# Part of a scan stage's front for batch 0 placed between the steps of the preceding stage's last chain

## The reference, cut to what matters

```python
# delta attention: 16 heads of 32, per head a state S (32 x 32)
pred = einsum('bhk,bhkv->bhv', kt, S)
delta = bt[..., None] * (vt - pred)
S = S + einsum('bhk,bhv->bhkv', kt, delta)
o = einsum('bhk,bhkv->bhv', qt, S)
...
og = o * gate, scaled per head by its rms; return og @ Wo.T

# selective scan: its first input is ctx_1024 (4, 512, 256), the gate z is the decoder's x
x = einsum('bld,ed->bel', hidden_states, in_proj_w)           # 256 -> 512 channels
xc = conv_general_dilated(x, conv_w, ...)                      # causal, 4 taps, per channel
x = silu(xc + conv_b)
dt_low, Bm, Cm = split(einsum('bdl,ed->bel', x, x_proj_w), [16, 32], axis=1)
dt = softplus(einsum('brl,dr->bdl', dt_low, dt_proj_w) + dt_proj_b)
state = state * exp(d * A) + (d * u) * b;  y = sum over 16 states of state * c
y = (y + D * x) * silu(z)
```

## Time and profile before

| what | value |
|---|---|
| median of 3 runs | 3259.52 us (3243.12 to 3270.23) |
| the profiled execution: its time, its span | 3257.45 us, 3255.7 us |
| its mean granted TensorE clock | 0.903 of full speed |
| busy over the span: PE, DVE, ACT, POOL | 82%, 59%, 44%, 35% |
| end of the last chain, from the span's start | 779.4 us |
| first scanned group of the scan | 860.4 us |

### The profile page before, as it was taken

The page is one execution under the profiler, slowest core; times in us unless marked ns, Lnnn a source line. Parts: engine busy times, 40 slices in busy tenths (PEclk is TensorE's granted clock), DMA queues, the critical chain, the costliest instruction groups (busy, mean ns, idle before and its releaser), DMA issues.

```text
span 3255.7 us, 50521 instructions
## 1 busy us (share of the span) xinstructions
PE 2679.7 (82%) x20154; PEld 1457.2 (45%) x20154; DVE 1923.6 (59%) x2994; ACT 1430.0 (44%) x2575; POOL 1130.8 (35%) x1056
## 2 busy tenths in 40 slices
PE   5788878876676766679998989888877999999788
PEld 3565655654222322248864544444443334333244
DVE  3323232333589899975735565665755666677377
ACT  3232333220544555433235445453622665666455
POOL 0443334440466666530005342526214233322000
PEclk8888898887888888789999999999887999999899
DMA  2222222230312314032244232333417444543301
GB/s 88 73 53 67 55 62 67 60 88 14 123 50 74 111 39 156 14 141 81 80 131 131 102 102 77 104 114 88 152 52 145 102 116 94 138 87 79 119 27 40
DMA packets 196766, 284.50 MB, mean 87 GB/s; under 512 B 84388, under 2 KB 86468, under 8 KB 195636
## 3 DMA queue, kind: packets, MB, share of 16 engines
q1 hardware_dynamic: 196532, 281.27, 29.5%
HBM read 192.08 MB, written 63.31 MB: 78 GB/s over the span
## 4 chain that ended last, share of the span: by engine, by line
PE 38%; DVE 9%; issue 4%; ACT 4%; POOL 2%; DMA 2%; SPq 1%; DVEq 0%; ACTq 0%; POOLq 0%
PE ps L236 8%; PE ps L3388 4%; PE ps L3401 4%; PE ps L1846 4%; PE ps L1857 4%; PE ps L3320 3%; PE ps L3337 2%; PE ps L3371 2%; PE ps L2512 1%; PE ps L3325 1%; DVE arena L2775 1%; DVE arena L1434 1%; DMA arena<-arena 1%; PE ps L2520 1%; DVE arena L2773 1%
## 5 line engine op out<-in xcount | busy, mean ns | idle before, releaser
L236 PE MATMUL ps<-arena 128*128 128x512 f32 (+3 forms) x1296 | 480.9, 525 | 16.1 <-ACT arena L2612 6.1
L3573 DVE TENSOR_REDUCE cross<-ps 128x1 f32<-128x512 f32 x512 | 327.6, 685 | 176.3 <-PE ps L3371 176.2
L1466 POOL TENSOR_TENSOR arena<-arena 128x1024 f32<-128x1024 f32 x128 | 311.1, 2431 | 193.1 <-DVE arena L1458 193.1
L3481 ACT ACTIVATE cross<-ps 128x512 f32<-128x512 f32 x512 | 276.7, 592 | 149.5 <-PE ps L3388 149.3
L1482 PE MATMUL ps<-arena 128*128 128x512 f32 x512 | 266.6, 661 | 56.6 <-POOL arena L1466 56.4
L1458 DVE TENSOR_TENSOR_SCAN arena<-ps,arena 128x1024 f32<-128x1024 f32 x128 | 291.3, 2277 | 33.1 <-ACT ps L1449 33.1
L236 PEld LDWEIGHTS ps<-arena 128*128 128x128 f32 (+2 forms) x1296 | 194.4, 155 | 254.0 <-issue 178.2
L1449 ACT ACTIVATE ps<-arena 128x511 f32<-128x511 f32 x256 | 165.1, 679 | 188.1 <-DVE arena L1458 187.9
L576 POOL TENSOR_TENSOR arena<-arena 128x31 f32<-128x31 f32 (+15 forms) x217 | 130.2, 600 | 324.6 <-DMA arena<-d_a 308.1
L1482 PEld LDWEIGHTS ps<-arena 128*128 128x128 f32 x512 | 104.4, 212 | 213.2 <-issue 125.5
L3388 PE MATMUL ps<-cross,cross 50*128 50x512 f32 x512 | 156.2, 505 | 28.4 <-ACT cross L3481 22.8
(11 more groups left out here) (351 smaller groups left out, 5171.2 us busy)
## 6 DMA issues: line engine op xcount, KB each, us to landing
arena<-d_bc SPq DMA_DIRECT2D x32, 1024.0 KB, 5.3
cross<-d_parts SPq DMA_DIRECT2D x192, 128.0 KB, 4.4
arena<-d_x SPq DMA_DIRECT2D x16, 1024.0 KB, 5.5
d_parts<-cross SPq DMA_DIRECT2D x32, 512.0 KB, 3.8
d_x<-arena SPq DMA_DIRECT2D x48, 256.0 KB, 2.7
arena<-in_D_wlm SPq DMA_DIRECT2D x12, 1024.0 KB, 6.4
d_signs<-arena SPq DMA_DIRECT2D x32, 256.0 KB, 2.2
arena<-arena SPq DMA_DIRECT2D x64, 128.0 KB, 2.1
```

The costliest lines, as they stand in the source:

```text
L236: ins = pe.e.matmul(ps[:m, :n], lhsT(k), rhs(k), start=(k == 0), stop=(k == chunks - 1))
L1466: pool.e.tensor_tensor(h, h, s.bc[:, turn % s.SLOTS, 1], ALU.mult).then_inc(*pool.up("scan_hC"))
L3481: act.e.activation(s.E[:, k % 2, j], s.rexp.bank((u, i)), ACT.Exp).then_inc(*s.rexp.empty(act, (u, i)))
L3573: dve.e.tensor_reduce(s.mx[:, u % 2, t, h:h + 1], s.rmax.bank((u, m)), AX.X, ALU.max, negate=True).then_inc(*s.rmax.empty(dve, (u, m)))
```

## The change

The scan's front of batch 0 (input projection, convolution, silu, and the projection to dt, B and C) moves out of the scan stage into Delta's last iteration. Each engine gets a `..._front` function of the scan: PE's is the generator that fills the last chain. It has 26 matmuls of 512 columns for the projection and convolution, an empty place, and 4 matmuls for dt, B and C: 31 pieces for 31 places. ACT's runs after `act_og` of pair 6, DVE's (the four multiplications with the taps) before the last chain, POOL's (the convolution of block 0) after its last inverse, SP's after the last `sp_inverse`: it stores the B and C rows and loads the first 3 of the 8 row pairs. The banks for these results come out of Delta's ring. So that the weights are there, `sp_next` is issued one iteration earlier, ahead of the last inverse's transfer. The buffers of the scan are laid out anew, so that those written early lie where Delta no longer reads. The gate's silu of batch 0 moves on ACT from ahead of the softplus to after the decay of group 2.

```diff
+            last = p == self.PAIRS - 1
+            if last:
+                yield from ((("in", c), "act") for c in range(2))
             if back:
                 yield ("o", p, 0), "dve"
             if front:
                 yield from ((("G", n, h), "act") for h in range(2))
                 yield from ((("PT", n, e), "dve") for e in range(2))
+            if last:
+                yield from ((("in", c), "act") for c in range(2, C))
+                yield ("xd",), "act"
...
-                s.sp_next(sp, s.dead, [s.ring.at_filled(sp, ("PT", s.PAIRS - 1, s.E - 1))])
+                s.next.sp_front(sp, s.ring)
...
                 for k in s.pieces(n):
                     s.sp_piece(sp, k)
+                if n == s.PAIRS - 1:
+                    s.sp_next(sp, s.dead, [s.ring.at_filled(sp, ("PT", n, s.E - 1))])
                 s.sp_inverse(sp, n)
...
+        s.next.pool_front(pool, s.ring, s.ring.at_filled(pool, ("PT", s.PAIRS - 1, s.E - 1)))
...
-            fill = s.pe_fill(pe, n) if front else iter(())
+            fill = s.pe_fill(pe, n) if front else s.next.pe_front(pe, s.ring) if p < s.PAIRS else iter(())
             if back:
                 s.pe_chain(pe, p, fill)
...
                 s.act_og(act, p - 1)
+            if p == s.PAIRS - 1:
+                s.next.act_front(act, s.ring)
             if front:
                 s.act_split_k(act, n)
...
                 s.dve_og_scale(dve, p - 1)
+            if p == s.PAIRS - 1:
+                s.next.dve_front(dve)
             if front:
                 s.dve_k_unit(dve, n)
...
+    def sp_front(self, sp, ring):
+
+        s = self
+        sp.e.wait_ge(*ring.at_emptied(sp, ("xd",)))
+        sp.e.dma_start(s.io["d_bc"][0].rearrange("a n l -> (a n) l"), s.xd[s.R:s.R + 2 * s.N, :]).then_inc(*sp.up("scan_bc_kept", 16))
+        for g in range(s.EARLY_ROWS):
+            s.sp_rows(sp, 0, g)
+        sp.b = 0
+
+    def pool_front(self, pool, ring, dead):
+
+        s = self
+        pool.e.wait_ge(*dead)
         pool.e.memset(s.up[:, :, 0:s.pad], 0.0).then_inc(*pool.up("scan_zeros"))
         pool.e.memset(s.ctx[:, :, 0:s.pad], 0.0).then_inc(*pool.up("scan_zeros"))
+        pool.e.wait_ge(*pool.at_all("scan_zeros"))
+        pool.e.wait_ge(*pool.at_all("scan_weights"))
+        pool.e.wait_ge(*ring.at_emptied(pool, ("in", 0)))
+        for k in range(s.K):
+            s.pool_tap(pool, 0, 0, k)
+        for k in range(1, s.K):
+            s.pool_add_tap(pool, 0, 0, k)
+        pool.b = 0
+
+    def pe_front(self, pe, ring):
+
+        s, e = self, pe.e
+        pe.e.wait_ge(*pe.at_all("scan_weights"))
+        pe.e.wait_ge(*pe.on("scan_ctx", 0))
+        for c in range(C):
+            pe.e.wait_ge(*ring.at_free(pe, ("in", c)))
+            if c == s.PE_CONV[0]:
+                pe.e.wait_ge(*pe.at_all("scan_taps"))
+                pe.e.wait_ge(*pe.at_all("scan_zeros"))
+            taps = (None,) if c in s.POOL_CONV else range(s.K)
+            for tap in taps:
+                for k in range(s.CC):
+                    if tap is None:
+                        lhsT, rhs = s.wi[:, k, c * P:(c + 1) * P], s.ctx[:, k, s.pad:]
+                    else:
+                        at = P * s.PE_CONV.index(c)
+                        lhsT, rhs = s.wk[:, tap, k, at:at + P], s.ctx[:, k, tap:tap + L]
+                    last = tap in (None, s.K - 1) and k == s.CC - 1
+                    ins = e.matmul(ring.bank(("in", c)), lhsT, rhs, start=(tap in (None, 0) and k == 0), stop=last)
+                    if last:
+                        ins.then_inc(*ring.fill(pe, ("in", c)))
+                    yield
+        yield
+        pe.e.wait_ge(*ring.at_free(pe, ("xd",)))
+        m = s.R + 2 * s.N
+        for c in range(C):
+            pe.e.wait_ge(*pe.on("scan_u", 0, c + 1))
+            ins = e.matmul(ring.bank(("xd",))[:m], s.wx[:, c, :], s.u[:, 0, c, :], start=(c == 0), stop=(c == C - 1))
+            if c == C - 1:
+                ins.then_inc(*ring.fill(pe, ("xd",)))
+            yield
+
+    def act_front(self, act, ring):
+
+        s = self
+        for c in range(C):
+            act.e.wait_ge(*ring.at_filled(act, ("in", c)))
+            dst = s.up[:, c, s.pad:] if c in s.POOL_CONV else s.dt[:, 0, c]
+            act.e.activation(dst, ring.bank(("in", c)), ACT.Copy).then_inc(*ring.empty(act, ("in", c)))
+        for c in range(C):
+            if c in s.POOL_CONV:
+                act.e.wait_ge(*act.on("scan_pool_conv", 0, s.POOL_CONV.index(c) + 1))
+            else:
+                act.e.wait_ge(*ring.at_emptied(act, ("in", c)))
+            act.e.activation(s.u[:, 0, c, :], s.dt[:, 0, c, :], ACT.Silu, bias=s.cb[:, c:c + 1]).then_inc(*act.up("scan_u"))
+        m = s.R + 2 * s.N
+        act.e.wait_ge(*ring.at_filled(act, ("xd",)))
+        act.e.activation(s.xd[:m, :], ring.bank(("xd",))[:m, :], ACT.Copy).then_inc(*ring.empty(act, ("xd",)))
+        act.b = 0
+
+    def dve_front(self, dve):
+
+        s = self
+        dve.e.wait_ge(*dve.at_all("scan_weights"))
+        for k in range(s.K):
+            dve.e.tensor_tensor(s.wk[:, k], s.wk[:, k], s.wi[:, :, P * s.PE_CONV[0]:], ALU.mult).then_inc(*dve.up("scan_taps"))
...
-        s.sp_keep_bc(sp, 0)
-        for g in range(s.G):
+        for g in range(s.EARLY_ROWS, s.G):
             s.sp_rows(sp, 0, g)
...
-        for c in s.POOL_CONV:
-            for k in range(s.K):
-                s.pool_tap(pool, 0, c, k)
-            for k in range(1, s.K):
-                s.pool_add_tap(pool, 0, c, k)
         s.pool_floor(pool, 0, 0)
         s.pool_dt(pool, 0, 0)
...
-        for c in range(C):
-            s.act_up(act, 0, c)
-        s.act_u(act, 0)
-        s.act_gate(act, 0)
-        s.act_xd(act, 0)
         s.act_abs(act, 0, 0)
         s.act_ln(act, 0, 0)
...
-                if b and k == 7:
+                if k == (7 if b else 1):
...
-        for c in range(C):
-            for half in (0, 1) if c in s.PE_CONV else (None,):
-                s.pe_in(pe, 0, c, half)
-        s.pe_xd(pe, 0)
         s.pe_dt(pe, 0, 0)```

On PE the last chain changes like this, from the transposes of pair 6 to the third step. Before:

```order
L679 MATMUL ps<-arena 128x128 x8
L777 MATMUL ps<-arena 128x128 x2
L767 MATMUL ps<-arena 32x128 x2
L777 MATMUL ps<-arena 128x128 x2
L767 MATMUL ps<-arena 32x128 x2
L777 MATMUL ps<-arena 128x128 x2
```

## The result

The changed kernel takes 3231.68 us (median of 6 runs, 3223.12 to 3235.8) against 3257.89 us for the kernel before (6 runs, 3243.12 to 3270.23): ratio 0.9919, 95% interval 0.9893 to 0.9945. That is 26 us, where 31.8 were forecast; the forecast ratio of 0.9902 lies inside the interval. The profiled execution of the changed kernel has a span of 3229.9 us, 25.8 less than before.

The account below looks back on a forecast made before the run. Strictly sequential stages bound the kernel, so time saved between last chain and first scan comes off the end; -35.2 + 1.0 + 4.8 + 0.5 - 2.9 = -31.8 us from 3259.52 gives 3228 us, range 3212 to 3245.

Parts of the forecast that it names:

- The front: Batch 0's work ahead of the first scan, taken out of the scan stage: first scan at 825.2 instead of 860.37, -35.2 us.
- The chain: Last chain on PE with matmuls in its gaps: 2.92 us a step, +1.0 per output, +4.8 us in all.
- rival (a): Before and in last chain: issue wait stays (+2.9), inverse's transfer queues (+2), chain starts at slow clock (+2.8); 3235.5 us, 22%.
- Rival (b): Last chain: filled, it never leaves the slow clock, 5.7 us a step, +43 us, time 3271 us; chance 5%.
- The early weights: Ahead of the last chain: weights issued before the inverse's transfer, +0.5 us for its queueing, -2.9 us for PE's issue wait.
- The stall's term: Line 669 in pair 7's triangles: PE's 5.26 us issue wait falls to 2.4 once the weights' traffic is gone, -2.9 us.
- The inverse's queueing: Pair 7's inverse transfer may wait behind the early weights' traffic: +0.5 us taken, bounds 0 and 3.
- The gate: ACT after decay 2: table load and silu take 3.2 us, 2.3 of it slack, so +1.0 us.
- Rival (c): More comes back: line 669 finds its instructions there (-2.4), output projection keeps the busier chain's clock (-2.6); 3223 us, 11%.

## Why the prediction was right

- **The front is worth 35 us, not its 27 us of matmuls.** Right, by the right mechanism. The next late thing was named (`wdt` behind the store of batch 3, then the slow matmul), and it came at 818.38: 9.5 us behind the output projection, 9.3 forecast, and took 2.04 us, 1.97 forecast. The experiment that removes it gives 8.1 us.
- **The chain.** The price per step was exact: 12 steps and three outputs from 736.86 to 774.90 are 38.0 us, by the forecast's numbers 12 x 2.92 + 3.0 = 38.0. Mis-sized were its ends: the first fill cost 1.6 us instead of 1.0, since it met the slow clock (1.91 us at 733.64), and the steps with the projection took 7.0 us for two where 6.2 were forecast. That slow first fill is all that came of rival (a)'s slow start of the chain, 0.6 of its 2.8 us. Rival (b), a chain that stays at the slow clock, is out: 1.00 from the first update on.
- **The early weights.** The stall's term was slightly small. Its cause, PE waiting for instructions that the weights hold up, fits the place of the instruction packet in all eleven traces. The Trainium skill (Runtime: NRT & Kernel Launch, Instruction fetch mechanics) has instruction fetch hidden, and by that the sum would have been -28.9 us. The traces differ from it: the stall follows the transfer's place in both directions, 5.26 to 2.12 us and 1.61 to 4.58. The inverse's queueing was +1.7 in this trace, more than the 0.5 taken and within the bound of 3, and mostly absent in others: the first part of rival (a) is out, its second happens now and then.
- **The gate.** The +1.0 for ACT's delay is seen in the kernel with the gate behind the logarithm. In the changed kernel the announced wait of DVE for ACT did not come; the step missed that a logarithm 3 us later meets POOL's instruction, and at group 3 the delay was 2.4 us. That only 0.6 of it was left at the end was not foreseen either, so that this term is near its forecast by luck. The sentence that DVE is busy without a gap from the first scan was wrong: it waits for ACT ahead of 12 scans of the stage, 33.1 us in all before and 32.4 after. ACT in turn waits for PE at some of these, and there a delay as well as a gain is partly taken back.
- **Rival (c)** did not come: 1.61 us of stall stayed, and the output projection took 16.12 us, 0.5 less than before, with the same idle time ahead of it. In the other traces it took 15.62 to 16.82 us with a filled chain or without, so even these 0.5 us need not be the change's.

The terms missed by -0.5, +1.2, -0.7, +1.4 and -0.4 us, which add up to +1.0 only because they partly cancel. What is left is 31 us in the stretch and 26 us in the medians. The part behind the scan, which the change leaves alone, moves by more than this difference from trace to trace.

## What to carry to other kernels

A chain of dependent small steps is room for independent work, and its price can be read where the same chain is already filled: take the filled step's length, not the sum of the matmuls. The place counts, not the mere earliness: the same work in one block gained nothing that could be measured. Then look what small thing the new start waits for, since it is cheaper to move than anything before it; and expect that a gain at the start of a pipelined stage is partly given back at a later wait for another engine.

## What the runs showed of the hardware

- Small useless matmuls can shorten a chain: without them the granted clock fell to 0.50 in parts of it and a step took 3.31 us there; with 128 columns in each 0.5 us gap the clock was 1.00 after the first steps and stayed there, and a step took 2.37 us.
- Four DVE multiplications of two arena operands (128x768) took 3.56 us with POOL idle (at 720.03 in the changed kernel) and 7.20 us at 810.02 in the kernel before, where POOL was working (line 1287 from 809.01).
- A bulk load of 2.7 MB that is still under way at a burst of 256 tiny matmuls lengthened PE's wait without a semaphore: 3.6 to 5.3 us in three traces, 1.5 to 2.4 in eight without it. The 0.02 MB packet on the instruction queue came 2.2 to 4.5 us after the burst's start instead of 1.4 to 1.9, and PE resumed 2.3 to 2.7 us after it in ten of the eleven.
- The last instruction of POOL's inverse, with hardly anything changed ahead of it, ended between 711 and 724 us in eleven executions.
